# Taking 22 zero products out of the waits of the image attention and of the first text term

## What is computed

```python
def _L0_tok_ref(input, ...):
    x = jnp.einsum('bchpwq,dcpq->bhwd', xp, patch_w) + patch_b     # 8 images of 64 tokens
    x = _layernorm(x, ln_g, ln_b) + _sinusoidal_pe(N, D)
    identity = x
    x = gelu(x @ ff1_w + ff1_b) @ ff2_w + ff2_b
    qkv = (x @ qkv_w + qkv_b).reshape(B, nW, WIN, 3, NH, dh)       # 12 heads of 16, windows of 64 tokens
    scores = jnp.einsum('bwqhd,bwkhd->bwhqk', q, k) * dh ** (-0.5)
    o = jnp.einsum('bwhqk,bwkhd->bwqhd', softmax(scores), v).reshape(B, N, D)
    x = o @ proj_w + proj_b + identity
    return x + ff(x)

def _L0_txt_ref(...):                                              # the text terms
    emb = words + domain @ proj_w.T + proj_b + types + pos
    return layernorm(emb) * ln_gamma + ln_beta

h = concatenate([tok, txt]); h = h + attention(layernorm(h)); h = h + experts(layernorm(h))
```

## Time and profile before

| | |
|---|---|
| median of 3 runs | 757.97 us (754.09 to 759.02) |
| the profiled execution: its own time | 751.9 us |
| its span, first to last instruction | 750.4 us |
| mean granted TensorE clock over the span | 0.997 |
| TensorE busy | 721.9 us, 96% of the span |
| VectorE, ScalarE, GpSimd busy | 302.1, 238.6 and 214.1 us |

### The profile page before, as it was taken

How to read it: one execution, slowest core, us unless ns; L and a number is a source line. 1 busy time by engine, 2 the same in 40 slices (tenths; PEclk the granted TensorE clock), 3 DMA queues, 4 the chain that set the end, 5 groups by cost and what they waited for, 6 DMA issues and landing times.

```text
span 750.4 us, 17659 instructions
## 1 busy us (share of the span) xinstructions
PE 721.9 (96%) x7212; PEld 534.3 (71%) x7212; DVE 302.1 (40%) x812; ACT 238.6 (32%) x515; POOL 214.1 (29%) x286
## 2 busy tenths in 40 slices
PE   7999899899999999899999999999999999999995
PEld 6447666677687777667546864789789788888654
DVE  1445576666466637634333742112211211111243
ACT  0202443655546546463243001121222122212110
POOL 5537115754132323200010057112112111211363
PEclk9999999999999999999999999999999999999998
DMA  8700000830000000000000045299999999894133
GB/s 304 275 0 2 3 0 2 287 106 3 1 2 14 2 2 14 2 1 12 1 1 12 1 163 204 83 410 372 353 344 372 337 355 379 333 358 169 32 85 84
DMA packets 34289, 102.80 MB, mean 137 GB/s; under 512 B 5034, under 2 KB 20399, under 8 KB 28849
## 3 DMA queue, kind: packets, MB, share of 16 engines
q1 hardware_dynamic: 24272, 70.29, 26.3%
q0 software_dynamic: 9952, 31.60, 11.4%
HBM read 90.66 MB, written 9.83 MB: 134 GB/s over the span
## 4 chain that ended last, share of the span: by engine, by line
PE 88%; DVE 5%; ACT 2%; issue 2%; another core or an unknown queue 1%; DMA 1%; POOL 0%; SPq 0%; DVEq 0%; ACTq 0%; POOLq 0%
PE PS L1625 14%; PE PS L1989 11%; PE PS L2422 9%; PE PS L2302 6%; PE PS L2426 5%; PE PS L2066 3%; PE PS L1863 3%; PE PS L2438 3%; PE PS L1877 2%; PE PS L2390 2%; PE PS L1631 2%; PE PS L2443 2%; PE PS L1903 2%; PE PS L1707 1%; PE PS L1922 1%
## 5 line engine op out<-in xcount | busy, mean ns | idle before, releaser
L1989 PE MATMUL PS<-X,w_sgu 64*128 64x512 f32 x432 | 98.6, 599 | 3.0 <-DVE gu L1457 1.2
L1583 DVE TENSOR_TENSOR rh<-rsg,PS 128x768 f32<-128x768 f32 x32 | 30.5, 955 | 158.3 <-ACT rsg L1021 158.3
L1989 PEld LDWEIGHTS PS<-X,w_sgu 64*128 64x128 f32 x432 | 40.8, 187 | 50.0 <-issue 44.5
L2422 PE MATMUL PS<-xt,w_rgu 128*128 128x128 f32 x576 | 70.1, 276 | 1.0 <-ACT rsg L1021 1.0
L2422 PEld LDWEIGHTS PS<-xt,w_rgu 128*128 128x128 f32 x576 | 67.5, 192 | 3.1 <-issue 3.1
L1021 ACT ACTIVATE rsg<-PS 128x768 f32<-128x768 f32 x32 | 26.0, 811 | 132.5 <-PE PS L2426 101.7
L678 POOL DMA_DIRECT2D y_slots<-ys x32 | 17.6, 551 | 155.2 <-ACT ys L1013 155.2
L1625 PE MATMUL PS<-w_rdn,rh 128*128 128x192 f32 x288 | 50.9, 327 | 0.0
L1625 PEld LDWEIGHTS PS<-w_rdn,rh 128*128 128x128 f32 x288 | 46.2, 190 | 0.4 <-issue 0.4
L832 ACT ACTIVATE pb<-sm,nm 128x128 f32<-128x128 f32 x144 | 42.4, 372 | 10.6 <-DVE nm L1372 10.5
L580 POOL TENSOR_TENSOR rs<-ve,minus_half 128x3 f32<-128x3 f32 x12 | 10.5, 871 | 118.1 <-DVE ve L1283 118.1
(11 more groups left out here) (376 smaller groups left out, 1394.8 us busy)
## 6 DMA issues: line engine op xcount, KB each, us to landing
w_rgu<-in_wgu SPq DMA_DIRECT2D x24, 1152.0 KB, 7.6
w_pgu<-in_wgu SPq DMA_DIRECT2D x16, 1152.0 KB, 7.3
w_rdn<-in_wd POOLq DMA_DIRECT2D x22, 576.0 KB, 6.6
w_pdn<-in_wd POOLq DMA_DIRECT2D x16, 576.0 KB, 6.3
x_slots<-zeros SPq DMA_DIRECT2D x1, 3072.0 KB
xs<-x_slots SPq DMA_DIRECT2D x32, 96.0 KB, 4.5
y_slots<-ys POOLq DMA_DIRECT2D x32, 96.0 KB, 5.8
w_sgu<-in_shared_gu SPq DMA_DIRECT2D x2, 1152.0 KB
```

The source lines that it names most:

```text
L1583: dve.tensor_tensor(rh[:, j, :], rsg[:, j, :], PS[:, 2:4, :].rearrange("p a b -> p (a b)")[:, 0:FF], ALU.mult).then_inc(S["r_h"], 1)
L1989: mm = pe.matmul(PS[:, bank, :], w_sgu[rows, e, c, 128 * m:128 * m + 128], X[rows, c, tokens], start=(c == 0), stop=(c == 2))
L2422: pe.matmul(dst(y, m), w[:, y, 128 * m:128 * m + 128], xt[:, j, y, :], start=(m % 4 == 0), stop=False, skip_group_check=True)
```

## The change

Eight calls of `spare` are deleted: four products ahead of the first text term's waits, and 5 + 4 + 3 + 2 + 1 + 1 + 2 = 18 products at seven places in the image attention. The waits that stood ahead of them stay where they are; they then stand directly ahead of the next step's own waits. The products at the start of the stream and those of the later block stay. Nothing else is touched.

```diff
             def text_terms(k):
                 if k < 2:
-                    if k == 0:
-                        spare(0, 4)
                     pe.wait_ge(S["t_dc"], k + 1)
                     pe.wait_ge(S["t_hot"], 1)
                     pe.wait_ge(ld_txt, 8 * 16)
...
             img_scores(0)
             pe.wait_ge(S["t_rd"], B)
-            spare(7, 5)
             img_scores(1)
             pe.wait_ge(S["a_sub"], 1)
-            spare(0, 4)
             img_scores(2)
             pe.wait_ge(S["a_sub"], 2)
             img_turn_weights(0)
-            spare(7, 3)
             img_outputs(0)
             img_scores(3)
             img_turn_weights(1)
             pe.wait_ge(S["a_on"], 1)
-            spare(7, 2)
             img_outputs(1)
             pe.wait_ge(S["a_sub"], IT)
             img_turn_weights(2)
             img_turn_outputs(0)
             img_turn_outputs(1)
-            spare(7, 1)
             img_outputs(2)
             img_turn_weights(3)
             img_turn_outputs(2)
-            spare(7, 1)
             img_outputs(3)
             pe.wait_ge(S["a_ptc"], IT)
-            spare(4, 2)
             img_turn_outputs(3)
```

## The result

The changed kernel takes 766.97 us (median of 4 runs, 763.0 to 769.73) against 758.19 us for the kernel before (median of 4): a ratio of 1.013, 95% interval 1.0088 to 1.0172. The forecast was 760.0 us with a range up to 766.5; what came lies just above the range, near the time of rival 2 (768.4 us).

The account below looks back on a forecast made before the run. TensorE, busy 96% of the span, was taken to bound the kernel. Two clock falls at 1.5 us less 0.95 us of schedule gain gave +2.05 us on 757.97: 760.0 us, range 754.5 to 766.5.

Parts of the forecast that it names:

- rival 2: Image stage: clock low throughout, +9.9 us, plus 1.5 at the text term, less 0.95: +10.4, 768.4 us; chance 0.13.
- The naive gain: Zero products (L1637), 20 to 100 us: the chain's whole share, 6.5 us, comes off, giving 751.5 us; chance 0.03.
- The later part of that step: Image attention, first outputs: they start about 0.95 us earlier, after first turns that start 0.99 us earlier.
- the gap had been foreseen: First text term: TensorE without work from about 22.2 to 23.85 us, 1.7 us; no time won there.
- the gaps around the turns of the first weights: Image attention, 72.2 to 75.87 us: two gaps of together 2.8 us within 3.7, where the clock may fall.
- The price of a fall: Clock falling ahead of dense work: 1.5 us lost per fall, 3.0 us as upper bound.
- the sum: Whole kernel: falls in two of three thinned places, 2 x 1.5 - 0.95 = +2.05 us.
- the row of the start: Kernel start: nine passes at the low level took 3.0 us instead of 1.6; low for the first 3.1 us.
- The prediction's own sign of being wrong: Whole kernel: clock at 1.00 from the start to 740 us, or low for longer than some 6 us at a time.
- Rival 1: Image attention: the clock holds and only the schedule changes, 0.95 us faster, 757.0 us; chance 0.36.
- the gap of 2.03 us: Ahead of the patch products: an idle gap that left the clock high, the twelve passes behind it taking 2.19 us.

## Why the prediction was wrong

**The naive gain was rightly refused.** The chain's 6.5 us for L1637 were not there. At the text term nothing was won, in the image attention 0.98 us up to the first turns (0.99 forecast). The later part of that step, 0.95 us at the first outputs, shrank to 0.32 us (81.80 - 71.97 against 76.82 - 66.67), because the turns already ran at the low level.

**The direction was right, and one of the two places.** The clock fell twice, as forecast, and near 24 us where the gap had been foreseen. That the second fall lies between 73 and 76 us is luck: the whole stage stood 5.3 us later by then. Counted from the first scores, the gaps around the turns of the first weights, from which the fall was forecast, begin 5.5 us behind them (72.2 - 66.67). The falls began earlier: 3.5 us behind them in the changed kernel, 2.7 in its second profile, 2.05 and 4.1 in the two profiles with the text products back, and two of these four without any gap. So those gaps are not what lowered the clock in the image attention.

**The price of a fall is the step that failed.** It stood in the sum as 1.5 us, with 3.0 as the upper bound, and measured 4.8 us at the text term and 6.8 us at the image attention and projection, or 7.8 us with the 0.98 us that it swallowed. With these the sum would have been 4.8 + 7.8 - 0.98 = 11.6 us. The 1.5 us came from the start of the kernel, where the engine ran full blocks of zero products, and was carried over with the sentence that the work behind the text term is dense because the chain there is almost all TensorE. Busy and dense are not the same: behind the text term TensorE was busy for 10.13 of 10.24 us, and the clock stayed at 0.50. The experiment with full blocks behind the wait shows that the row of the start was read rightly and used in the wrong place: there, too, the clock was back after 3.4 us. In every fall of these profiles it came back 3.0 to 5.6 us into a longer run of full blocks, and what comes ahead of such a run was missing from the price: 5.0 us of text terms (24.37 to 29.36), and in the image attention everything up to the projection, 24.3 us (75.46 to 99.77). The low level lasted 6.8 to 10.2 us at the text term and 27 to 31 us in the image attention. The prediction's own sign of being wrong, a clock that is low for longer than some 6 us at a time, came at both places.

**Rival 2 had the mechanism, and was put aside by a wrong argument.** I wrote that at half the rate TensorE looks busier, which should bring the clock back. In the stretch at the low level it was busy for 22.34 of 27.31 us, and with small products in the waits for 33.67 of 34.14 us, and the clock didn't come back. That its total nearly came true is in part luck, since two of its terms were off in opposite directions. The low level in the image stage was priced too high: its steps slow down by less than 1.9 (scores 1.75 to 2.81, outputs 0.89 to 1.48, turns 0.87 to 1.54 us, the projection 3.05 to 4.51), and with these its own sum is 4 x 0.59 + 1.06 + 3 x 0.67 + 1.46 = 6.9 us instead of 9.9. The fall at the text term was priced too low, 1.5 us instead of 4.8. Low clock through the image stage with a fall at the text term was given 0.13 and left out of the range.

**Rival 1** (the clock holds) rested on the gap of 2.03 us. Behind the same gap, 1.91 us there, the clock was lost in another execution, so that row showed one outcome of several.

**What the timings can't show.** Lengths in a profile are of one execution. The 11.6 and 11.3 us of the two profiles lie above the 9.9 us (interval 6.7 to 13.0) and 9.1 us (6.0 to 12.2) that the two ratios give, within the intervals. Falls differ in length from one execution to the next, and from the second feed-forward to the first product of the experts' gates both profiles are 0.5 us shorter than before (298.7 against 299.25 us), the second one another 1.5 us behind that; what shortens them was not tried.

## What to carry to other kernels

Taking a filler instruction off the critical chain isn't a gain until what it holds up elsewhere is priced. And the price of a fallen clock is not the rise at the start of a kernel: it is read from the work that follows, up to the next run of full blocks. Ask of a stretch not only whether TensorE is busy, but with what: here full blocks, zero products or turns, held the clock, and a stretch of mostly small products, busy for 99% of its time, stayed at the low level throughout.

## What the runs showed of the hardware that was not expected

- The clock fell to 0.50 where TensorE had had no gap: at 68.49 us behind 3.41 us of the values' and scores' products, at 72.65 us in the second profile of the changed kernel, and at 70.68 us behind 3.48 us of scores and small zero products.
- It stayed at 0.50 for 34.1 us in which TensorE was busy 33.67 us with small products, turns, 17-column outputs and, in the last 4.9 us, the projection.
- Under full blocks it was back after 3.4 us: under zero products (25.83 to 29.24, 68.58 to 71.99, and 69.27 to 72.68 with the next scores at its end) and under the patch products (8.76 to 12.18).
- The same code kept the clock in one execution and lost it in another: the start gap of some 2 us (1.00 in the earlier trace rows, 0.50 from 8.76 us in the run with full blocks), and the first scores of the kernel before (all slices at 9 tenths or more in the earlier trace rows, 0.50 from 68.58 and 69.27 us in two kernels that are the same up to there).
- At the low level a pair of passes of 512 columns took 2.08 us instead of 1.12, a tile's scores of 16x64 2.8 us instead of 1.75, only 1.6 times.
